# A two-layer graph kernel on one core: GpSimd's edge program unrolled, 20 and 8 slots for gathered rows, indices loaded from ScalarE's queue

## What is computed

```python
h = jnp.maximum(_layernorm(x, axis=-1), 0.0)
# layer 0: rows dst gathered, weighted, multiplied by W, summed into rows src
support = jnp.einsum('ni,oi->no', h, W)
x = x + jax.ops.segment_sum(support[dst] * edge_weight[:, None], src, num_segments=N)
h = jnp.maximum(_layernorm(x, axis=-1), 0.0)
# layer 1: rows src gathered, summed into rows dst, then a two-layer MLP on every node
agg = jax.ops.segment_sum(h[src], dst, num_segments=N)
h1 = (agg + h) @ W1 + b1                       # 256 -> 1024
h1 = relu((h1 - mean(h1)) * rsqrt(var(h1) + 1e-5) * gamma + beta)
x = x + relu(h1 @ W2 + b2)                     # 1024 -> 256
```

## Time and profile before

| | us |
|---|---|
| median of 3 runs | 4067.0 |
| lowest, highest | 4066.32, 4071.11 |
| span of the profiled execution, first to last instruction | 4058.6 |
| GpSimd busy | 1034.4 (801 instructions) |
| TensorE busy, weight loads | 3538.1, 3016.0 |
| VectorE, ScalarE busy | 2172.7, 2170.4 |
| mean granted TensorE clock | 0.937 of full |

### The profile page before, as it was taken

How to read it: one execution, slowest core, us unless ns; L and a number is a source line. 1 busy time by engine, 2 the same in 40 slices (tenths; PEclk the granted TensorE clock), 3 DMA queues, 4 the chain that set the end, 5 groups by cost and what they waited for, 6 DMA issues and landing times.

```text
span 4058.6 us, 59233 instructions
## 1 busy us (share of the span) xinstructions
PE 3538.1 (87%) x17911; PEld 3016.0 (74%) x17911; DVE 2172.7 (54%) x5226; ACT 2170.4 (53%) x3631; POOL 1034.4 (25%) x801
## 2 busy tenths in 40 slices
PE   0377777677878869999999999999999999999999
PEld 0366666566767657778888888888888888888888
DVE  0255555466666658855545555455555554554554
ACT  0254445332222259956665666656666656566665
POOL 2188888778888820000000000000000000000000
PEclk9788888888888889999999999999999999999999
DMA  7877777567777789932221221212212112122120
GB/s 267 292 168 191 192 172 184 89 162 164 160 162 164 161 255 359 359 133 63 63 76 62 72 68 62 78 62 66 73 62 76 64 62 78 62 68 71 62 78 31
DMA packets 172385, 516.97 MB, mean 127 GB/s; under 512 B 25983, under 2 KB 78202, under 8 KB 166426
## 3 DMA queue, kind: packets, MB, share of 16 engines
q1 hardware_dynamic: 97082, 413.69, 29.9%
q0 software_dynamic: 75264, 102.81, 14.9%
HBM read 361.58 MB, written 206.03 MB: 140 GB/s over the span
## 4 chain that ended last, share of the span: by engine, by line
PE 57%; POOL 20%; issue 10%; DMA 6%; ACT 5%; SPq 1%; DVE 1%; POOLq 0%; ACTq 0%; another core or an unknown queue 0%; DVEq 0%
PE ps_a L1204 27%; PE ps_b L1218 18%; PE ps_b L1219 9%; POOL x_table L510 7%; POOL agg_table L510 7%; POOL arena L504 6%; ACT arena L625 4%; DMA x_table<-in_x 4%; PE ps_a L1188 2%; DMA agg_table<-arena,scatter_now 1%; ACT arena_r L643 1%; SPq L384 1%; DMA x_table<-arena,scatter_now 0%; DMA arena<-in_x,gather_now 0%; PE ps_a L1167 0%
## 5 line engine op out<-in xcount | busy, mean ns | idle before, releaser
L1218 PE MATMUL ps_b<-w_hl,arena_r 128*128 128x512 f32 x3128 | 1140.7, 399 | 0.1
L1035 DVE TENSOR_TENSOR arena_r<-arena,arena_r 128x512 fp32r<-128x512 f32 (+1 forms) x784 | 539.9, 689 | 958.0 <-ACT arena_r L682 958.0
L677 ACT ACTIVATE arena<-ps_a,bn_bias,bn_scale 128x512 f32<-128x512 f32 (+1 forms) x784 | 607.2, 774 | 781.4 <-PE ps_a L1204 781.4
L1204 PE MATMUL ps_a<-arena_r,w_hi 128*128 128x512 f32 x3136 | 982.2, 394 | 1.5 <-DVE arena_r L1027 1.5
L1219 PE MATMUL ps_b<-w_hl,arena_r 128*128 128x256 f32 x3128 | 876.5, 280 | 0.0
L1218 PEld LDWEIGHTS ps_b<-w_hl,arena_r 128*128 128x128 f32 x3128 | 587.5, 188 | 134.5 <-issue 0.4
L1204 PEld LDWEIGHTS ps_a<-arena_r,w_hi 128*128 128x128 f32 x3136 | 540.8, 188 | 109.5 <-ACT arena_r L668 1.9
L1204 PE MATMUL ps_a<-arena_r,w_lo 128*128 128x512 f32 x1568 | 610.9, 390 | 0.0
L1219 PEld LDWEIGHTS ps_b<-w_hl,arena_r 128*128 128x128 f32 x3128 | 589.8, 189 | 26.7
L682 ACT ACTIVATE arena_r<-arena 128x512 fp32r<-128x512 f32 (+1 forms) x784 | 495.1, 631 | 71.6
L742 DVE BATCH_NORM_STATS2 row_stats<-arena 128x6 f32<-128x256 f32 x392 | 137.8, 414 | 562.5 <-DMA arena<-in_x,gather_now 333.4
(11 more groups left out here) (118 smaller groups left out, 4302.3 us busy)
## 6 DMA issues: line engine op xcount, KB each, us to landing
x_in<-x_table SPq DMA_DIRECT2D x291, 512.0 KB, 3.8
arena<-agg_table SPq DMA_DIRECT2D x194, 512.0 KB, 5.2
x_table<-in_x SPq DMA_DIRECT2D x10, 5000.0 KB, 31.7
agg_table<-zeros SPq DMA_DIRECT2D x40, 1250.0 KB
out<-zeros SPq DMA_DIRECT2D x97, 512.0 KB, 6.0
arena<-in_x,gather_now POOLq DMA_INDIRECT x196
x_table<-arena,scatter_now POOLq DMA_INDIRECT x196
arena<-x_table,gather_now POOLq DMA_INDIRECT x196
```

The costliest lines, as they stand in the source:

```text
L677: act.activation(hid[m % 2][:, 0:w], ps_a[:, 2 + m % 2, 0:w], ACT.Relu, scale=bn_scale[:, m:m + 1], bias=bn_bias[:, m:m + 1]).then_inc(hid ...
L1035: dve.tensor_tensor(hid_lo[m % 4][:, 0:w], hid[m % 2][:, 0:w], hid_hi[m % 4][:, 0:w].bitcast(F32), ALU.subtract).then_inc(hid_lo_ready, 1)
L1204: ins = pe.matmul(ps_a[:, 2 + m % 2, 0:w], w_part[:, kb, cols], h_part[:, kb, 0:w], start=(t == 0), stop=(t == len(terms) - 1))
L1218: pe.matmul(ps_b[0:p, r, :], hid_hi[m % 4][:, cols], w2, start=(m == 0), stop=(m == MB - 1), skip_group_check=True)
```

## The change

1. **GpSimd.** Its program is unrolled: no loop, no registers. A gather reads its indices straight from `gather_ids`; `gather_now` and VectorE's copies go. Layer 0 has a ring of 20 slots for gathered rows, layer 1 one of 8 (RING). 22 groups (88 gathers) go ahead of layer 0's first accumulate, 8 groups (32) ahead of layer 1's (LEAD). The rest, 108 and 164 gathers, are dealt evenly over the first 45 turns (SPREAD), each portion between the accumulates of a turn and the wait for them.
2. **Loads.** The index and weight loads and W go to ScalarE's queue, each load as 112, 15 and 1 rows in place of 127 and 1. The `dst` indices that layer 0 gathers by come first, with a semaphore of their own, which GpSimd waits for; VectorE waits for three other loads; layer 1's gather indices come last. SP issues copy pieces 0 and 1 back to back.
3. **W1 and W2** are loaded behind layer 0 into slots of the ring that layer 1 doesn't use, and VectorE splits them after its eighth turn of layer 1.
4. **Loop bodies.** ScalarE's and VectorE's loops have 20 turns (layer 0) and 8 (layer 1) in a body. `pick_info` moves behind the statistics. SBUF is laid out anew.

In the diff GROUPS is 49, QUAD 4, AHEAD 4.

```diff
+    EVEN_ROWS = FULL_EDGE_ROWS // 16 * 16
+    LOAD_PARTS = 16 * 3
+    RING = (20, 8)
+    LEAD = (22, 8)
+    SPREAD = GROUPS - 4
...
             copy_piece(0)
-
-            sp.wait_ge(ids_blank, 1)
-            def load_edges(tile, ids):
-                sp.dma_start(tile[0:FULL_EDGE_ROWS, :],
-                             ids[0:FULL_EDGE_ROWS * COLS].rearrange("(p c) -> p c", c=COLS)).then_inc(ids_loaded, 16)
-                sp.dma_start(tile[FULL_EDGE_ROWS:P, 0:LAST_EDGES],
-                             ids[FULL_EDGE_ROWS * COLS:E].rearrange("(p c) -> p c", p=1)).then_inc(ids_loaded, 16)
-            for i, ids in ((1, dst), (0, src)):
-                load_edges(gather_ids[i], ids)
-                load_edges(target_ids[i], ids)
-            load_edges(weights, edge_weight)
-            sp.dma_start(w_rows[:, :, :], W.rearrange("(b p) i -> p b i", p=P)).then_inc(w_loaded, 16)
+            copy_piece(1)
             sp.wait_ge(consts_ready, 1)
...
-            for i in range(1, COPY_PIECES):
+            for i in range(2, COPY_PIECES):
                 copy_piece(i)
...
+            with sp.Fori(0, ZERO_PIECES) as i:
+                zero_piece(i)
+            load_vectors()
             sp.wait_ge(layers[0].retired, GROUPS + AHEAD)
+            load_w1()
+            load_w2()
...
+            def gather(l, op):
+                g, a = op // QUAD, op % QUAD
+                if a == 0 and g >= l.ring:
+                    pool.wait_ge(l.normed_ready, g - l.ring + 1)
+                    pool.sem_inc(pool_gate, 1)
+                pool.indirect_dma_start(ring[g % l.ring][:, a, :], None, l.gather_from,
+                                        bass.IndirectOffsetOnAxis(ap=l.gather_ids[:, op:op + 1], axis=0)
+                                        ).then_inc(l.gathered[g % l.ring], 16)
...
+            def gathers_before(l, t):
+                return QUAD * l.lead + min(t, SPREAD) * QUAD * (GROUPS - l.lead) // SPREAD
+            pool.wait_ge(ids_blank, 3)
+            pool.wait_ge(dst_loaded, LOAD_PARTS)
             for l in layers:
-                for g in range(AHEAD):
-                    pool.wait_ge(l.gather_ready, g + 1)
-                    gather(l, Turn(0, 0, g))
-                gather_next(l, Turn(0, 0, AHEAD))
+                if l.n == 1:
+                    pool.wait_ge(src_loaded, LOAD_PARTS)
+                for op in range(QUAD * l.lead):
+                    gather(l, op)
...
-                turns(pool, GROUPS, 2, AHEAD + 1, lambda t: step(l, t))
+                for t in range(GROUPS):
+                    scatter(l, t)
+                    if t < GROUPS - 1:
+                        for op in range(gathers_before(l, t), gathers_before(l, t + 1)):
+                            gather(l, op)
+                    pool.wait_ge(l.scattered[t % 2], (t // 2 + 1) * (16 * QUAD))
+                    pool.sem_inc(l.retired, 1)
...
         def _(act):
+            def load_edges(tile, ids, loaded):
+                for p0, p1, cols in ((0, EVEN_ROWS, COLS), (EVEN_ROWS, FULL_EDGE_ROWS, COLS), (FULL_EDGE_ROWS, P, LAST_EDGES)):
+                    act.dma_start(tile[p0:p1, 0:cols], ids[p0 * COLS:p0 * COLS + (p1 - p0) * cols].rearrange(
+                        "(p c) -> p c", c=cols)).then_inc(loaded, 16)
+            act.wait_ge(ids_blank, 1)
+            load_edges(gather_ids[1], dst, dst_loaded)
+            act.wait_ge(ids_blank, 2)
+            load_edges(target_ids[0], src, info_loaded)
+            load_edges(weights, edge_weight, info_loaded)
+            act.dma_start(w_rows[:, :, :], W.rearrange("(b p) i -> p b i", p=P)).then_inc(w_loaded, 16)
+            act.wait_ge(ids_blank, 3)
+            load_edges(target_ids[1], dst, info_loaded)
+            load_edges(gather_ids[0], src, src_loaded)
...
-            dve.wait_ge(ids_loaded, 16 * 10)
+            dve.wait_ge(ids_blank, 3)
+            dve.wait_ge(info_loaded, 3 * LOAD_PARTS)
...
+                SPLIT_AT = 8
+                first = (1, SPLIT_AT)[l.n]
+                for t in range(first):
+                    edge_step(l, Turn(0, 0, t))
+                if l.n == 1:
+                    dve.wait_ge(w12_loaded, 16 * 6)
```

More of the change, by code:

```diff
@@ new lines, in gnn_program @@
+        normed = [carve(arena, EDGE_AT + s * SLOT, QUAD, D)[0] for s in range(2)]
+        message = [carve(arena, EDGE_AT + (2 + s) * SLOT, QUAD, D)[0] for s in range(2)]
+        targets_sb = [carve(arena, EDGE_AT + 4 * SLOT + s * QUAD * P, QUAD * P)[0] for s in range(2)]
+        work_r = WEIGHTS_R
+        same = [carve(arena_r, work_r + s * QUAD * QUAD * P, QUAD, QUAD * P)[0] for s in range(2)]
+        same_diagonal = [arena_r[:, work_r + s * QUAD * QUAD * P:][:, 0:QUAD * (QUAD + 1) * P].rearrange(
+            "p (a x) -> p a x", a=QUAD)[:, :, 0:P] for s in range(2)]
@@ L216, in __init__ @@
                 self.info_ready = sem(f"info_ready_L{n}")
[L217 to L218 removed]
+                self.ring = RING[n]
+                self.lead = LEAD[n]
+                self.gathered = [sem(f"gathered_L{n}_{s}") for s in range(RING[n])]
                 self.moments_ready = sem(f"moments_ready_L{n}")
@@ L303, in below, with turns @@
                 return self.per > 0 or 0 <= self.base < end
-        def turns(eng, total, head, tail, step, loop=None):
+        def turns(eng, total, head, tail, step, loop=None, per=AHEAD):
             for t in range(head):
                 step(Turn(0, 0, t))
-            passes = (total - head - tail) // AHEAD
+            passes = (total - head - tail) // per
             def body(i):
-                for u in range(AHEAD):
-                    step(Turn(i, AHEAD, head + u))
+                for u in range(per):
+                    step(Turn(i, per, head + u))
             if loop:
@@ L318, in turns @@
                     body(i)
-            for t in range(head + passes * AHEAD, total):
+            for t in range(head + passes * per, total):
                 step(Turn(0, 0, t))
@@ L912, in _, with edge_pass @@
                 edge_step(l, Turn(0, 0, -1))
-                turns(dve, GROUPS, 1, AHEAD + 2, lambda t: edge_step(l, t),
-                      loop=lambda passes, body: looped(passes, AHEAD * (EDGE + NODE * l.n), body))
+                SPLIT_AT = 8
[4 more added lines that the diff above has]
+                    dve.wait_ge(w12_loaded, 16 * 6)
+                    chain.then(dve.tensor_copy(w1_hi, w1_f))
+                    chain.then(dve.tensor_copy(w2_hl[:, :, 0, :], w2_f))
+                    chain.wait()
+                    dve.tensor_tensor(w1_lo, w1_f, w1_hi.bitcast(F32), ALU.subtract)
+                    dve.tensor_tensor(w2_hl[:, :, 1, :], w2_f, w2_hl[:, :, 0, :].bitcast(F32),
+                                      ALU.subtract).then_inc(w12_split, 1)
+                passes = (GROUPS - first - (AHEAD + 2)) // l.ring
+                def edge_pass(i):
+                    for u in range(l.ring):
+                        edge_step(l, Turn(i, l.ring, first + u))
+                looped(passes, l.ring * (EDGE + NODE * l.n), edge_pass)
+                for t in range(first + passes * l.ring, GROUPS):
+                    edge_step(l, Turn(0, 0, t))
             dve.wait_ge(node_std_ready, 1)
```

156 lines of the change are left out of this document (58 added, 98 removed).

## The result

| | before | after | ratio, 95% interval |
|---|---|---|---|
| median of 4 runs | 4066.88 us | 4047.68 us | 0.9955 [0.9943, 0.9967] |
| lowest, highest | 4066.32, 4071.11 | 4045.29, 4051.17 | |
| profiled execution, span | 4058.6 us | 4045.5 us (its time 4048.41) | |
| medians of a later comparison, 7 and 4 runs | 4061.6 us | 4034.29 us | 0.993 [0.9914, 0.9947] |

By the two profiled executions the gain is 13.1 us: layer 0 is over 20.5 us earlier, layer 1 takes 9.1 us longer, the node stages 1.7 us less.

What follows compares the result with a forecast made beforehand. GpSimd's issue was taken to bound the edge stages. Layer 0 at -27.7 and layer 1 at -8 us took the 4058.6 us span to 4023; plus 8.4 for the median, 4031 us, own range 4010 to 4052, with rivals 3966 to 4066.

Steps and rivals of the forecast that it cites:

- The copy: Start of layer 0: with pieces 0 and 1 issued at once, the copy of x ends at 167 us, 21 us earlier.
- The index loads: Start of layer 0: each load row waits for a copy row; gathers from 33 us, other loads at 168, first accumulate 198.5.
- Rival 2: Start of layer 0: index loads pass quickly beside the copy, second turn at 198 instead of 209, 4021 us; chance 0.12.
- The turn of layer 0: Zeroing piece meets the third and fourth accumulates, adding 2.0 us to a bare 10.3: 12.3 us against 12.85; layer 0 -27.7 us.
- 4 x 10.8 = 43, last four 4 x 10.4: End of layer 0: four turns of 10.8 us after the 40 with zeroing, then last four of 10.4 us, 42 together.
- Layer 1: 642 us plus 2 for node loads, against 651.9 before: -8 us.
- Nothing, at most those 7 us: Layer 1, turn 8: VectorE's split of W1 and W2 costs nothing, at most 7 us if the lead is gone.
- the lead's own term: Layer 1: 32 gathers ahead in place of 20, 41 us to the first accumulate, not 33, covering 7.2 us of idle time.
- At no cost: Unrolled GpSimd code keeps 0.30 us before a gather; dropped gather_now copies, TensorE, new SBUF places and loop bodies cost nothing.
- Rival 3: Start of layer 0: GpSimd can't have 80 gathers under way, first accumulate at 232, 4064 us, no change; chance 0.1.
- rival 1: Turns of layer 0: the zeroing piece doesn't meet the accumulates, turns of 10.8, 60 us less, 3971 us; chance 0.2.
- rival 4: Turns of layer 0: the piece's full 3.7 us enter each landing wait, turns of 14.0, 68 us more, 4099 us; chance 0.08.

Runs made afterwards that it cites:

- Run 5: The change with a lead of 5 groups in layer 0, the rest dealt over 44 turns: 4038.72 us, 0.9943 of the kernel before.
- Run 1: The change with each agg_table zeroing piece issued when a turn is retired, not when rows are normed: 3978.57 us, 0.979 of the kernel before.
- run 8: The kernel before with only the zeroing moved, piece i waiting until group i is retired: 4065.02 us against 4061.6.
- run 9: The change with the zeroing moved to retirement, a lead of 5 groups in layer 0 and 44 turns of dealing: 4042.78 us, 0.9944 of the kernel before.
- run 7: The change with layer 0's gathers dealt over 40 turns in place of 45: 4030.21 us, against 4034.29 for the change beside it.
- run 10: The kernel of Run 1 with gathers dealt from the front, none in each layer's last five turns: 3980.47 us, 0.9794 of the kernel before.
- first two batches: The first eight follow-up kernels, four per batch, beside the kernel before at 4062.39 us and 4061.6 us.
- Run 3: The change with a lead of 5 groups in layer 1 instead of 8: 4045.54 us, one run.
- run 6: The change unaltered, measured again on another batch's chip: 4034.29 us, 0.993 of the kernel before.
- last batch: The last three follow-up kernels: run 9, Run 1's kernel again (3985.19 us) and run 10, beside the kernel before at 4065.02 us.
- run 4: The change with index loads and W on SP's queue between copy pieces 0 and 1, still as 112, 15 and 1 rows: 4036.42 us, one run.

## Why the prediction was right and where it failed

The sign, the mechanism of layer 0's turns and the range were right, the size was not: 4031 forecast, 4047.7 measured. The forecast of the span was 4022.9, it was 4045.5. The 22.6 us are the -9, +12, +5 and +17 below, less 1.7 for the node stages and rounding; 6.2 of them come back in the medians, since the forecast put 8.4 us on top of the span and the changed kernel's median lies 2.2 above its own. That the time lies in the forecast's own range, 4010 to 4052, is in part luck: without the 9 us that the loads gained it would be near 4057.

- **The copy, right.** It was to end at 167; the first accumulate, which waits for it, goes out at 173.5 in this profile and at 167.0 to 169.9 in those of the experiments. Run 5 shows the worth of this part: 20 of its 23 us.
- **The index loads, wrong, -9 us.** "I take the upper one, since these rows are no gathered bundles": 33 us for the first load, 168 for the rest. It was 19 and 115. Rival 2 described the course: accumulates from the end of the copy, held behind the gathers, second turn at 198; it began at 200.0 (forecast: 209.3). The rule from the Trainium skill, "DMA: Bandwidth & Descriptors", section "Queues, rings and completion order", by which a DMA engine takes turns between queues by the packet and not by the row, points the right way: at 3.3 us for a copy row the first load took the time of five or six rows, not nine, and the four together that of 35, not 52 (my estimate, from 19.3 and 115.2 us). That a part of a load passes in a single turn is not shown. The backlog, 65 gathers at 167 us by the transfers' records where 63 were forecast, drained in about 26 us; 30 were forecast.
- **The turn of layer 0, right in kind, undersized, +12 us.** The piece was to come 5.1 us into the turn and did (205.10 against 200.01). Of the range of 0 to 3 us for what it adds to the bare turn of 10.3 I took 2.0; it was 2.2 (12.54), of which 1.9 are the longer wait behind the fourth accumulate (5.1 us against 3.2) and 0.3 the four accumulates themselves. 39 turns make 9 us of that, turn 41 the other 3 (14.9 us), where SP issues the vector loads behind the last piece. The 5.1 us of landing against 3.5 are the collision as the records have it. Run 1 takes it away, and in runs 5, 8 and 9 it isn't there.
- **"4 x 10.8 = 43, last four 4 x 10.4", wrong, +5 us.** The even dealing over 45 turns hands the last gathers out four turns ahead, and the lead of 22 groups has run down by then. I checked what the lead gives at the start and never what it is at the end. Runs 5, 7 and 10 show this step.
- **Layer 1, wrong in sign, +17 us.** It was to be 8 us shorter and is 9 longer. 8.7 us are the start: "41 us to the first accumulate" is what the first two batches show, 41.2 to 41.8; here it took 49.7. The other 8.4 are the turns, 611.4 us for 49 in place of 603. "Nothing, at most those 7 us" for the split of W1 and W2 in turn 8 left out what it does to GpSimd (below; some 2 us in this profile), and the lead of eight runs down to four here too. Turn by turn against the prices 12.85, 11.56 and 10.7 us, turns 1 to 8 are 3.8 us over, 9 to 39 3.4 and 40 to 48 4.4; the last is 1.2 under, and 2 were allowed for. Which of the 3.4 are node loads is not shown. Run 3 shows that the lead's own term, some 8 us, was right.
- **At no cost: confirmed.** The gap between unrolled instructions is 0.30 us as in the loop. **Rival 3 refuted**: 88 gathers went out without a stall. **Rivals 1 and 4**: turns of 12.5 lie between their 10.8 and 14.0; run 1 is rival 1 made true, at 3978.6 where it gave 3971.

## What to carry to other kernels

Work that covers a wait is not free to move: before gathers are taken out from under an accumulate's landing, look at what else enters the DMA engines at that moment of the turn, and give bulk writes a trigger at the phase where nobody waits. Reckon a lead at its end as well as at its start; dealt evenly over one turn too many it falls short just where it is needed. And where two edits each show nothing, try them together, if one can bring about what the other takes away: here they were worth 0 and 4 us apart and 58 together.

## What the runs showed that I had not expected

**GpSimd issues more slowly while VectorE splits W1 and W2.** In the change's run 6, GpSimd in layer 1:

```profile
892.10 0.95 POOL L486 DMA_INDIRECT arena<-x_table,gather_ids  x1 [0.30 <-issue]
893.35 2.66 POOL L486 DMA_INDIRECT arena<-x_table,gather_ids  x1 [0.30 <-issue]
896.32 3.39 POOL L495 DMA_INDIRECT agg_table<-arena,scatter_now  x1 [0.31 <-issue]
900.01 1.87 POOL L495 DMA_INDIRECT agg_table<-arena,scatter_now  x1 [0.30 <-issue]
902.19 1.66 POOL L495 DMA_INDIRECT agg_table<-arena,scatter_now  x1 [0.31 <-issue]
```

VectorE in the same microseconds:

```profile
893.54 1.21 DVE L901 CAST arena_r<-arena 128x2048 fp32r<-128x2048 f32 x1
894.68 1.21 DVE L902 CAST arena_r<-arena 128x2048 fp32r<-128x2048 f32 x1
895.92 2.29 DVE L904 TENSOR_TENSOR arena_r<-arena,arena_r 128x2048 fp32r<-128x2048 f32 x1
898.13 2.28 DVE L905 TENSOR_TENSOR arena_r<-arena,arena_r 128x2048 fp32r<-128x2048 f32 x1
```

A gather takes 2.66 us instead of 0.95 and an accumulate 3.39 instead of 1.6 while VectorE works on 2048 columns, 3.5 us in this turn, in 6.9 us of such work. Before, the split fell between the layers and met two accumulates that took 2.2 us. The Trainium skill, "SBUF — State Buffer", section "SBUF: two separate sides", has a mechanism: VectorE, in some of its operations, and GpSimd take a shared pair of ports under an exclusive lock, and GpSimd can't write the descriptors of its transfers while VectorE has it. The rows agree with that in kind, though GpSimd lost only half of the 6.9 us; which of the four operations would hold the lock no run here shows, and none moves the split away.

**A start of layer 1 that differs by 8 us.** In the profile after, VectorE, in the stretch from 23 to 45 us behind the layer's first gather:

```profile
827.05 0.16 DVE L796 SCALAR_TENSOR_TENSOR shift<-ps_a,info_now 128x4 f32<-128x4 f32 x1 [1.20 <-issue]
832.15 0.38 DVE L820 BATCH_NORM_AGGREGATE chunk_moments<-node_stats 128x2 f32<-128x6 f32 x4 [4.94 <-issue]
834.13 0.16 DVE L758 SCALAR_TENSOR_TENSOR row_norm<-row_moments,row_norm 128x4 f32<-128x4 f32 x1 [1.60 <-remote]
836.96 0.16 DVE L803 TENSOR_TENSOR scatter_now<-shift,info_now 128x4 int32<-128x4 f32 x1 [2.67 <-remote]
```

Ten such gaps of 0.5 to 4.9 us follow one another, on TensorE too (2.36 and 1.87 us), where the profile of run 6 has none that ends with "issue" or "remote". It is there in the profile after and in all three of the last batch, and in none of the six of the other two batches with a lead of eight in layer 1; the three batches ran on three chips, one each; which of them the profile after is from, if any, I can't tell. The profile names no transfer at the end of these gaps. The kernel before has three such gaps in its profile too, 0.27 to 2.65 us, 22 to 26 us behind its first gather, and the kernel of run 8 has none: so the gaps are not the change's alone. Whether the chip or the placement of the code decides is open, and I did not try it.

**The form of the loads, not their queue, held the copy.** In run 4 the index loads stand on SP's queue between copy pieces 0 and 1, as before, but in parts of 112, 15 and 1 rows:

```profile
1.61 1.36 SPq L372 DMA_DIRECT2D gather_ids<-in_dst  x3
...
7.07 7.80 SPq L372 DMA_DIRECT2D gather_ids<-in_src  x3
14.91 0.52 SPq L367 DMA_DIRECT2D x_table<-in_x  x1
```

All of them are issued by 14.9 us, where the loads of 127 rows and one held SP until 37.5 us, and the copy behind them until 38.9. The wait of 15.1 us in the first of those isn't of their making: by the transfers' records no row of a load moves before 17 to 18 us in either kernel, as copy piece 0 goes first. But then the 635 rows of 784 bytes, 40 ns each, take from 18.3 to 41.4 us before and from 17.0 to 21.5 in run 4. That is one behind the other before, and the mean DMA share of 0.07 from 18.5 to 38.9 us is about that of one of 16 engines; in run 4 five or six must go at a time (estimates from those numbers). So the form of the loads decides. The order of the loads differs as well, and whether it is the multiple of 16 rows or just another number of them is not shown. The queue decides something else: the same loads in the same form are complete at 115 us from ScalarE's queue, beside the copy, and at 22.0 from SP's, ahead of piece 1. Both leave the end of the copy where it is (first accumulate at 167 to 170 in the experiments).
